# A latent-attention layer on one core: the first stage software-pipelined, own tiles first, head 1's weights prepared in unit 0

## What is computed

```python
xn = layernorm(x)                                  # 2048 x 512
q = xn @ wq                                        # 16 heads x (128 nope + 64 rope)
kva = xn @ wkv_a                                   # 128 latent + 64 rope
ckv = kva[..., :128] * rsqrt(mean(kva[..., :128]**2) + 1e-6) * kv_norm_scale
kv = ckv @ wkv_b                                   # per head: 128 k_nope, 128 v
q_pe, k_pe = rope(q_pe), rope(kva[..., 128:])
scores = (q . k) * 192**-0.5, causal mask, softmax
out = x + (attn @ v) @ wo + xn @ sum_r(factors[r]) / sqrt(8) + bias
```

## Time and profile before

| | us |
|---|---|
| median of 3 runs | 1527.58 (1526.75 to 1527.88) |
| the profiled execution | 1529.43 |
| its span, first to last instruction | 1527.5 |
| busy: PE, DVE, ACT, POOL | 1479.1, 1012.5, 974.4, 904.7 |

### The profile page before, as it was taken

How to read it: one execution, slowest core, us unless ns; L and a number is a source line. 1 busy time by engine, 2 the same in 40 slices (tenths; PEclk the granted TensorE clock), 3 DMA queues, 4 the chain that set the end, 5 groups by cost and what they waited for, 6 DMA issues and landing times.

```text
span 1527.5 us, 25754 instructions
## 1 busy us (share of the span) xinstructions
PE 1479.1 (97%) x7908; PEld 758.3 (50%) x7908; DVE 1012.5 (66%) x2563; ACT 974.4 (64%) x2418; POOL 904.7 (59%) x905
## 2 busy tenths in 40 slices
PE   5789999999999999999999999999999999999997
PEld 4444455555544544444445454545545555455553
DVE  6666777767777766655455565656656666676786
ACT  6777676777767476666466667665646666654553
POOL 1367777775655455666465656566645655664552
PEclk9999999999999999999999999999999999999998
DMA  6369989998776588787677677886856677854654
GB/s 219 105 124 206 205 181 189 187 189 163 150 154 139 114 174 168 142 175 138 131 143 139 134 139 146 153 162 134 155 117 138 136 140 149 157 133 98 120 119 99
DMA packets 646598, 227.83 MB, mean 149 GB/s; under 512 B 599360, under 2 KB 612160, under 8 KB 646080
## 3 DMA queue, kind: packets, MB, share of 16 engines
q1 hardware_dynamic: 646464, 226.20, 73.0%
HBM read 65.67 MB, written 17.83 MB: 55 GB/s over the span
## 4 chain that ended last, share of the span: by engine, by line
PE 80%; ACT 7%; DVE 6%; issue 3%; POOL 3%; DMA 1%; SPq 0%; POOLq 0%; ACTq 0%; DVEq 0%
PE ps L390 16%; PE ps L391 16%; PE ps L392 16%; PE ps L534 6%; PE ps L539 6%; PE ps L540 6%; PE ps L536 6%; PE ps L535 6%; ACT ex L774 3%; POOL st L1341 1%; DVE gm L1123 1%; DVE ps L1125 1%; POOL q L1332 1%; DMA st<-x_in 0%; ACT sqr L695 0%
## 5 line engine op out<-in xcount | busy, mean ns | idle before, releaser
L1341 POOL TENSOR_TENSOR st<-ex,st 128x512 f16<-128x512 f32 (+3 forms) x640 | 637.7, 1015 | 504.3 <-ACT st L784 494.5
L774 ACT ACTIVATE ex<-ps,nm,scales 128x512 f32<-128x512 f32 (+3 forms) x640 | 452.5, 709 | 466.8 <-DVE nm L1142 452.8
L1123 DVE TENSOR_REDUCE gm<-ps 128x1 f32<-128x512 f32 (+1 forms) x384 | 249.0, 669 | 176.8 <-PE ps L540 172.6
L784 ACT ACTIVATE st<-ex 128x512 f16<-128x512 f32 (+3 forms) x640 | 341.4, 561 | 5.9
L534 PE MATMUL ps<-kTh,q 128*128 128x512 f16 (+3 forms) x640 | 223.2, 349 | 8.5 <-ACT ex L774 8.4
L539 PE MATMUL ps<-kRh,q 128*128 128x512 f16 (+3 forms) x640 | 222.9, 348 | 4.5 <-POOL q L1332 4.5
L390 PE MATMUL ps<-pT,vH 128*128 128x512 f16 (+3 forms) x640 | 222.4, 347 | 2.4 <-DMA pT<-st 2.4
L536 PE MATMUL ps<-kTh,q 128*128 128x512 f16 (+3 forms) x640 | 223.0, 348 | 0.0
L535 PE MATMUL ps<-kTl,q 128*128 128x512 f16 (+3 forms) x640 | 223.0, 348 | 0.0
L540 PE MATMUL ps<-kRl,q 128*128 128x512 f16 (+3 forms) x640 | 223.0, 348 | 0.0
L391 PE MATMUL ps<-pT,vH 128*128 128x512 f16 (+3 forms) x640 | 222.5, 348 | 0.0
(11 more groups left out here) (200 smaller groups left out, 2145.2 us busy)
## 6 DMA issues: line engine op xcount, KB each, us to landing
wA<-w_abs SPq DMA_DIRECT2D x48, 256.0 KB, 3.0
wV<-w_vo SPq DMA_DIRECT2D x48, 256.0 KB, 3.0
pT<-st SPq DMA_TRANSPOSE x640, 3.3
fland<-factors_in SPq DMA_DIRECT2D x28, 256.0 KB, 3.3
wP<-w_pe SPq DMA_DIRECT2D x24, 256.0 KB, 3.0
wsq<-wq_in SPq DMA_DIRECT2D x16, 256.0 KB, 3.9
wso<-wo_in SPq DMA_DIRECT2D x16, 256.0 KB, 3.1
w_abs<-wA SPq DMA_DIRECT2D x16, 256.0 KB, 2.3
```

The costliest lines, as they stand in the source:

```text
L774: e.activation(ex[:, n % NEX, 0:keys], s_bank(n)[:, 0:keys], ACT.Exp, bias=nm[:, (i * QT + r) % 4:(i * QT + r) % 4 + 1], scale=scales[:, p ...
L784: e.activation(stage(n, keys)[:, :, 0, :], ex[:, n % NEX, 0:keys].rearrange("p (t n) -> p t n", n=P), ACT.Copy).then_inc(z["a_pH"], 1)
L1123: e.tensor_reduce(m, b, AX_X, ALU.max).then_inc(z["v_max"], 1)
L1341: e.tensor_tensor(s[:, :, 1, :], ex[:, n % NEX, 0:keys].rearrange("p (t n) -> p t n", n=P), s[:, :, 0, :], ALU.subtract).then_inc(z["g_pL" ...
```

## The change

The loops of the first stage run to NT + 8 and each step lags its producer further: the normalized tile is transposed two steps after ACT wrote it, latent products come two steps behind the transposes, `latent` four, `latent_scale` six, the keys' transposes eight. `xn` is now `ex` (four buffers) instead of `rot` (two); latent products use four banks. Tiles are worked off in the order given by `PAIRS`: chunk 3's first, then chunks 0, 1, 2. Head 0's q and rope are computed inside the loop, the first two pieces of the first scores at its end, ahead of the last keys. The values' high halves move from ACT to POOL. The weights and q of head 1 move from the first stage into the fills of unit 0. The first load of x is two DMAs, each pair has a semaphore of its own, and the loads and stores are reordered for it. `bank_order` follows the new order of PE (left out here), and semaphore names are added.

```diff
+PAIRS = tuple(QT * c // 2 + n for c in (ORDER[0],) + tuple(range(NC - 1)) for n in range(QT // 2))
...
+def tile(n):
+    return 2 * PAIRS[n // 2] + n % 2
+def both(p):
+    return slice(2 * PAIRS[p], 2 * PAIRS[p] + 2)
...
     out = []
+    if i == 0:
+        out += [[("tq", 1), ("tkv", 1), ("sq1", 2)], [("wabs", 1), ("nrm", 2), ("wpe", 2)],
+                [("q", 1), ("tq", 2), ("tkv", 2), ("wpe_low", 2)], [("wabs", 2)]][r]
...
+        xn = ex
...
-                    e.wait_ge(z["v_kva"], t // 2 - 1)
-                    e.wait_ge(z["a_kk"], t // 2 - 1)
+                if t // 2 >= SBANKS:
...
-                elif n == 0:
-                    e.wait_ge(z["v_kva"], NP)
-                    e.wait_ge(z["a_kk"], NP)
-                    e.wait_ge(z["v_kT"], NP)
+                if n < SBANKS:
+                    e.wait_ge(z["v_kva"], NP - SBANKS + 1 + n)
+                    e.wait_ge(z["a_kk"], NP - SBANKS + 1 + n)
+                if i == 0 and r == 0 and p < NC - 1:
...
             e.wait_ge(z["g_const"], 1)
-            for t in range(NT + 4):
-                p = t // 2
+            norm(("na", 0), ("a_sqa",), nra[:, :])
+            for t in range(NT + 8):
                 if t < NT:
                     transpose_x(t)
-                if t == 0:
-                    norm(("na", 0), ("a_sqa",), nra[:, :])
+                if 0 <= t - 2 < NT:
+                    latent_product(t - 2)
+                if t % 2 == 0 and 0 <= t - 8 < NT:
+                    keys(t // 2 - 4)
                 if t == 7:
                     norm(("nrm", 0), ("a_sqp", "a_sq0", "a_sq1", "a_r8"), nrm[:, :])
-                if t in (8, 11):
-                    wq_transpose(t // 3 - 2)
-                    kv_transpose(t // 3 - 2)
-                if t in (10, 13):
-                    w_abs(t // 3 - 3)
-                if 0 <= t - 2 < NT:
-                    latent_product(t - 2)
-                if t % 2 == 1 and 0 <= p - 2 < NP:
-                    keys(p - 2)
+                if t == 11:
+                    wq_transpose(0)
+                    kv_transpose(0)
+                if t == 12:
+                    q_rope(0)
+                if t == 14:
+                    w_abs(0)
                 if t == NT + 1:
-                    q_rope(0)
-                if t == NT + 2:
                     q_latent(0)
-                if t == NT + 3:
-                    q_latent(1)
+                if t == NT + 5:
+                    scores(0, 0, 0)
+                    scores(0, 0, 1)
             for i in range(NU + 2):
                 for r in range(QT):
                     if i < NU:
-                        for p in range(chunk(i) + 1):
...
-            def value_parts(p2):
-                ts = slice(2 * p2, 2 * p2 + 2)
-                e.wait_ge(z["a_kk"], p2 + 1)
-                e.activation(vH[:, ts, :], kt[p2 % 4][:, :, 0:LORA], ACT.Copy).then_inc(z["a_vH"], 1)
...
             e.wait_ge(z["g_const"], 1)
             norm_scale(0)
-            normalize(0)
-            norm_scale(1)
-            e.wait_ge(z["d_wa"], 16)
-            square_sum(wa_f.rearrange("p k n -> p (k n)"), 0, nra[:, :]).then_inc(z["a_sqa"], 1)
-            for t in range(NT + 4):
-                p = t // 2
-                if t + 1 < NT:
-                    normalize(t + 1)
-                if t < NT:
+            for t in range(-2, NT + 8):
+                if t % 2 and 1 <= (t + 3) // 2 < NP:
+                    norm_scale((t + 3) // 2)
+                if t % 2 and 0 <= t - 9 < NT:
+                    keys((t - 9) // 2)
+                if t % 2 == 0 and 0 <= t - 4 < NT:
+                    latent((t - 4) // 2)
+                if 0 <= t < NT:
                     transpose_x(t)
+                if t % 2 == 0 and 0 <= t - 6 < NT:
+                    latent_scale((t - 6) // 2)
+                if t + 2 < NT:
+                    normalize(t + 2)
+                if t == -2:
+                    e.wait_ge(z["d_wa"], 16)
+                    square_sum(wa_f.rearrange("p k n -> p (k n)"), 0, nra[:, :]).then_inc(z["a_sqa"], 1)
                 if t == 0:
...
-                if t % 2 == 0 and 0 <= p - 2 < NP:
-                    latent_scale(p - 2)
-                    value_parts(p - 2)
-                if t == 3:
+                if t == 1:
                     e.wait_ge(z["a_sqa"], 1)
                     squares("sqk", 0)
+                if t == 2:
+                    squares("sq1", 0)
+                if t == 5:
+                    squares("sqp", 0)
+                if t == 6:
                     squares("sq0", 0)
-                if t == 5:
-                    squares("sq1", 0)
-                    squares("sqp", 0)
-                if t == 12:
+                if t == 8:
                     w_pe(0)
-                if t == NT + 3:
+                if t == NT + 1:
+                    rope_parts(0)
+                if t == NT + 2:
                     q_latent(0)
-                if t % 2 == 1 and 0 <= p - 2 < NP:
-                    keys(p - 2)
-                if t % 2 == 1 and 0 <= p - 1 < NP:
-                    latent(p - 1)
-                if t % 2 == 1 and p + 2 < NP:
-                    norm_scale(p + 2)
-            q_latent(1)
-            rope_parts(0)
-            for kind in ("sqk", "sqp", "sq0", "sq1"):
+            for kind in ("sqk", "sqp", "sq0"):
                 squares(kind, 2)
             for i in range(NU + 2):
                 for r in range(QT):
...
-                                if kind in ("q", "wo", "parts", "sqv"):
+                                if kind in early:
                                     fill(kind, n)
                     for p in range(0 if i == 0 else max(last, 0), last + 1):
                         high_parts(i, r, p)
                     for kind, n in fills(i, r):
                         if soon and kind == "pv":
...
                             continue
-                        if last < 2 or r >= 2 or kind not in ("q", "wo", "parts", "sqv"):
+                        if last < 2 or (r >= 2 and i) or kind not in early:
...
             norm_stats(0)
-            norm_scale(0)
-            norm_stats(1)
-            norm_scale(1)
-            for t in range(NT + 4):
-                p = t // 2
-                if t % 2 == 0 and 0 <= p - 2 < NP:
-                    latent(p - 2)
-                if t < NT:
+            for t in range(-4, NT + 8):
+                if t % 2 == 0 and 0 <= t - 4 < NT:
+                    latent((t - 4) // 2)
+                if t == 7:
+                    scale_pair(0)
+                if 0 <= t < NT:
                     transpose_x(t)
-                if t == 0:
+                if t == 12:
+                    q_rope(0)
+                if t % 2 == 0 and 0 <= (t + 4) // 2 < NP:
+                    norm_scale((t + 4) // 2)
+                if t == -2:
                     scale_latent()
-                if t == 1:
+                if t % 2 == 0 and 0 <= t - 8 < NT:
+                    keys((t - 8) // 2)
+                if t % 2 == 0 and (t + 6) // 2 < NP:
+                    norm_stats((t + 6) // 2)
+                if t == -2:
...
                 if t == 4:
...
-                if t == 7:
-                    scale_pair(0)
-                if t in (8, 11):
-                    wq_transpose(t // 3 - 2)
-                    kv_transpose(t // 3 - 2)
-                if t in (10, 13):
-                    w_abs(t // 3 - 3)
-                if t == 13:
+                if t == 9:
                     w_pe(0)
-                if t == NT + 2:
-                    q_rope(0)
-                if t == NT + 3:
+                if t == 11:
+                    wq_transpose(0)
+                    kv_transpose(0)
+                if t == NT - 1:
+                    w_abs(0)
+                if t == NT + 1:
                     q_latent(0)
-                if t % 2 == 1 and 0 <= p - 2 < NP:
-                    keys(p - 2)
-                if p + 2 < NP:
-                    if t % 2 == 0:
-                        norm_stats(p + 2)
-                    else:
-                        norm_scale(p + 2)
-            q_latent(1)
             for i in range(NU + 2):
...
+                    if (i, r) == (0, 3):
+                        q_latent(1)
                     for kind, n in sorted(fills(i, r), key=lambda work: SOON.get(work[0], len(SOON)) if 1 <= i < H else 0):
-                        fill(kind, n)
+                        if (kind, n) != ("q", 1):
+                            fill(kind, n)
...
                 e.tensor_tensor(fsum[:, k4, :], fsum[:, k4, :], fland[:, n % 2, :], ALU.add).then_inc(z["g_fac"], 1)
-            def value_parts(p2):
-                ts = slice(2 * p2, 2 * p2 + 2)
-                e.wait_ge(z["a_vH"], p2 + 1)
-                e.tensor_tensor(vL[:, ts, :], kt[p2 % 4][:, :, 0:LORA], vH[:, ts, :], ALU.subtract).then_inc(
-                    z["g_vL"], 1)
+            def values_high(p2):
+                e.wait_ge(z["a_kk"], p2 + 1)
```

(60 more changed lines are left out.)

94 lines of the change are left out of this document (48 added, 46 removed).

## The result

The changed kernel takes 1513.24 us (median of 4 runs, 1511.4 to 1514.25) against 1527.16 (1526.46 to 1527.88, 4 runs) for the kernel before: a ratio of 0.9907 with a 95% interval of 0.9890 to 0.9925, 13.9 us less. Forecast were 1509.6 us with a range of 1503.5 to 1519.5, and faster with a chance of 0.93. The profiled execution took 1514.25 us with a span of 1512.4, where 1509.5 was forecast and 1527.5 measured before.

What follows compares the result with a forecast made beforehand. PE was taken to bound the kernel from 97.66 us on, something else before. Gains of 11.8 + 7.4 less 1.2 gave 18.0 us: span 1509.5, median 1509.6 us, range 1503.5 to 1519.5.

Steps and rivals of the forecast that it cites:

- rival c: From 97.66 to 170 us DMA, not PE, sets the pace, so time stays within 3 us of 1527.6; chance 0.03.
- Last keys: First stage: with longer lags ACT sets the pace, and the last keys come at 58.7 instead of 70.5, 11.8 us.
- the gaps on the way: First stage: ACT still idles 3 us, a third of its some 9 us of waits between 15 and 66 us.
- From the last key to the first exponential: End of first stage: own tiles first leaves 3.1 us behind the last key instead of 10.5, a 7.4 us gain.
- The table load: Before the first exponential: ACT's 1.283 us load just hides by the row; by the skill page, 1.0 us more in total.
- POOL: First stage: eight casts of 0.67, 5.4 us, are free except at the end; cost 0 to 2, taken as 0.5.
- Head 1's weights in unit 0: Unit 0: 3.9 us of PE work moved in partly fills idle time; bounds 0 and 3.9, taken as 1.2 us.
- rival (b): Start waits and half clock around 76 to 86 us vanish, unit 0's extra work free: 1501 to 1504.5; chance 0.09.
- The sign of being wrong: Unit 0: PE idle over 3 us from first exponential to the second unit's end would show it dearer than taken.
- SP's queue: Unit 0: head 3's wq load lands about 66.0, ACT's squares arrive at 65.0; cost 0 to 1 us with slack.
- (a): First stage: the lag doesn't remove the gaps between engines, so the time is 1516 to 1520; chance 0.22.
- (d): First stage: TensorE stays at half clock, last keys 13 us later than before, 1534 us in all; chance 0.03.

Runs made afterwards that it cites:

- the swap: The changed kernel with head 2's transposes ahead of head 1's q in unit 0: 1510.77 us, ratio 0.9882 to the kernel before.
- The last kernel: Changed kernel plus the swap, second tile normalized before second pair's root, x's second pair loaded before wkv_a, last keys transposed before second scores piece: 1507.41 us.

## Why the prediction was right, step by step

*What bounds the kernel.* Right. From unit 1's first exponential on, both kernels need the same time to within 0.3 us (58.17 + 1360.30 and 58.22 + 1360.00), so a shift of the start passes through unchanged; DMA (rival c) took none of it. That PE would be full from 79 us on was not so: it waited 2.15 us up to 84.08 and ran at half clock from 85.3 to 88.7.

*Last keys, 11.8 us forecast, 9.9 measured.* The mechanism was right. ACT was busy for 88% from 15 to 55 us (35.33 of 40), over the 85% given, but that sign says little, as it was 83% before (33.33). Its wait for DVE's products fell from 5.5 to 0.7 us, and without the lag the keys come 4.1 later. The term that was mis-sized is the gaps on the way, drain included: 3 + 1 us forecast, and from 15 us to ACT's last key step ACT was idle for 6.5 (the waits that the profile names are 5.9, and 10.7 up to the last keys before). By the sum: ACT started at 5.36 instead of 5.85, was busy for 45.1 us up to 59.85 instead of 45.5, and was idle for 2.8 up to 15 us instead of 2.5 and for 6.5 behind it instead of 4. 5.36 + 45.1 + 2.8 + 6.5 + 0.8 = 60.6. One reading of the rows was too simple: of PE's 15.6 us of waits for ACT's tiles, 10.0 are its first two waits (7.53 and 2.50, up to 14.69 us), which stand behind the loads of x and not behind a link one step too young. The idea behind the 3, that the fullest engine runs through once its neighbours are a step ahead, holds by half: ACT's extra work costs 0.35 to 0.55 of itself.

*Four buffers.* The forecast said that they add no instruction and remove waits on a younger use, and gave them no price. For the latents that was the largest single condition of the gain, 10.2 us (the order of the tiles 6.9, the lag 6.0); for the normalized tiles it was nothing. These amounts overlap and don't add up. The sum did not suffer, since both are part of the change, but the edit with the largest weight had no term.

*From the last key to the first exponential, 3.1 forecast, 2.73 measured.* Right, 7.7 us of gain instead of 7.4, and the experiment with tiles in natural order puts 4.9 of it on the early scores and q, the clock's part included.

*The table load.* It hides, as the row said: its end and the row maximum's lie 0.09 us apart. The Trainium skill, "ScalarE: Activation LUTs", section "What ACT_TABLE_LOAD costs", adds about 1.38 us of drain to the 1.28 of the load. The traces don't show it: where the exponential is ready, it starts 0.13 us behind the load's end here, as the maximum comes in (63.21, 63.34) and 0.02 in the kernel with head 1's q late (68.51 + 1.28 = 69.79, 69.81). Nor is there a gap ahead of the load: in the changed kernel the instruction ahead of it ends at 61.91 (61.72 + 0.19) and the load starts at 61.93. The measurement decides for the row.

*POOL.* A cast took 0.40 us, within the bounds of 0 and 0.67, and nobody waited for the split of q at the end. POOL's eight casts and their subtractions, in the columns of the earlier trace rows:

```profile
L1290 POOL TENSOR_TENSOR vL<-kt,vH 128x256 f16<-128x256 f32 x8 | 5.4, 670 | 0.3
L1286 POOL CAST vH<-kt 128x256 f16<-128x256 f32 x8 | 3.2, 397 | 0.0
```

*Head 1's weights in unit 0, 1.2 us forecast, 2.8 measured.* This is the step that failed in size, though within its bounds of 0 and 3.9. The item was named rightly, q of head 1 behind row 2, but not how it costs. I priced PE's delay of a microsecond ahead of row 3's scores; row 3's exponentials come only 0.16 us earlier with the swap. The cost lies behind them: the next item takes the bank in which q lies, DVE empties it behind row 3's maxima, PE waits 2.15 us, and the clock falls behind that. From row 1's first exponential on, unit 0 became 4.4 us longer (20.4 to 24.8): 2.3 by the wait, 1.7 by the clock, 0.4 by the rest. Ahead of it, it became 1.7 shorter, as the half clock in the scores of row 1 is gone; the sum had no term for that, only rival (b). So the 2.8 are a balance, and that they lie this near to 1.2 is partly luck. With one entry moved in the list, unit 0 is 1.25 us shorter than before the change (26.82 against 28.07); that is the clock's 1.7 less some 0.4 for the additional work. The sign of being wrong, PE idle by more than 3 us in unit 0, came (30.84 - 26.57 = 4.3), but the kernel before had 3.9 there.

*SP's queue.* Right in what mattered: ACT's squares after the first row started at 66.06 without a wait, where the load was forecast for 66.0 with ACT at 65.0.

*The sum.* 9.9 + 7.7 - 2.8 = 14.8 against a forecast of 11.8 + 7.4 - 1.2 = 18.0; the span fell by 15.1. The median lies 1.0 below the profiled execution, not 1.85, which is most of the rest of the distance between 1509.6 and 1513.24.

*The rivals.* (a), the gaps stay, is half true: ACT's named waits went from 10.7 to 5.9, and the time lies between the forecast and it. (b) didn't happen as a whole, though one of its terms did: the half clock from 76 to 79 us and from 83 to 86 is gone. The last kernel, with unit 0's wait gone and the start's used, comes to 1507.4, still above its 1504.5. (d), half clock in the stage, did not happen: the clock was 1.00 in it.

## What to carry to other kernels

When each step of a pipeline over in-order engines is made to lag further, count for every buffer how many iterations lie between its writer and the one that empties it: where both fall into the same iteration, the lag is worse than none (1523.4 us here against 1519.2), and where another wait already contains the buffer's, more buffers are worthless. Work that was moved into a later unit cost here by its place and not by its amount: each item put into a rotation of banks changes the bank of every item behind it, so ask who held the bank that an item gets, and behind what its last reader stands in its own queue. A wait that is long isn't therefore dear: DVE's 1.90 us cost 0.16. To put first the tiles that the first consumer needs was worth as much as the whole lag (6.9 and 6.0 us in the medians), since it empties the stretch behind the last key, where little overlaps.
